# Second routing: the dense expert 0 becomes a routed expert, and 32 products of constants stand in the return's wait

## The reference

```python
logits = xf @ w_g                                   # 2048 x 8
topv, topi = jax.lax.top_k(logits, 2)
probs = softmax over the two chosen
capacity = int(2 * 1.25 * 2048 / 8)                 # 640
rank = cumsum over the first choices, then the second ones
mask = mask * (rank < capacity)
exp_batches = ... tokens of each expert, 8 x 640 x 128
h = gelu(exp_batches @ c_fc[e])                     # 128 -> 512
exp_out = h @ c_proj[e]                             # 512 -> 128
out = sum over the two experts, probability times exp_out
```

## Time and profile before

| what | value |
|---|---|
| median of 3 runs | 583.71 us (583.6 to 588.45) |
| span of the profiled execution, first to last instruction | 595.4 us |
| mean granted clock of TensorE over the span | 0.891 |
| PE busy | 505.9 us |
| DVE, ACT, POOL busy | 324.2, 239.9, 242.2 us |
| bytes moved, mean rate | 47.52 MB, 80 GB/s |

### The profile page before, as it was taken

One profiled execution on the slowest core, in us unless ns is written; L12 is line 12 of the kernel. 1 busy time (PEld: TensorE's weight loads), 2 busy tenths in 40 slices (PEclk: granted clock), 3 DMA queues, 4 the chain that ended last, 5 costly groups with the idle time before them and its releaser, 6 DMA issues.

```text
span 595.4 us, 9229 instructions
## 1 busy us (share of the span) xinstructions
PE 505.9 (85%) x3310; PEld 408.7 (69%) x3310; DVE 324.2 (54%) x1125; ACT 239.9 (40%) x477; POOL 242.2 (41%) x354
## 2 busy tenths in 40 slices
PE   3698993889769978978836799989899999999997
PEld 2557492778556626776725689988653779799997
DVE  4867338743896724598520246532774964433334
ACT  3643833233245541345520153322246187334430
POOL 5772957264334013475767306555390250000000
PEclk9799996569768998985668889999999799999999
DMA  9999801110850067400111122110800000000002
GB/s 285 334 176 196 260 34 35 37 39 28 294 153 1 1 185 219 128 1 2 44 46 48 44 68 65 55 35 24 274 2 0 2 1 2 0 1 1 1 2 70
DMA packets 55822, 47.52 MB, mean 80 GB/s; under 512 B 6059, under 2 KB 46201, under 8 KB 55649
## 3 DMA queue, kind: packets, MB, share of 16 engines
q1 hardware_dynamic: 52688, 41.54, 25.6%
q0 software_dynamic: 2656, 4.88, 2.6%
q10 hardware_dynamic: 432, 0.52, 0.3%
HBM read 34.69 MB, written 12.82 MB: 80 GB/s over the span
## 4 chain that ended last, share of the span: by engine, by line
PE 63%; DVE 20%; issue 4%; DMA 4%; POOL 3%; ACT 3%; another core or an unknown queue 3%; ACTq 0%; DVEq 0%; SPq 0%; POOLq 0%
PE ps L1244 10%; PE ps L1180 6%; PE ps L1063 4%; PE ps L1064 4%; PE ps L1065 4%; DVE st L1622 4%; PE ps L703 3%; PE ps L816 3%; PE ps L1091 2%; PE ps L756 2%; PE ps L746 2%; PE ps L839 2%; PE ps L819 2%; PE ps L1161 2%
## 5 line engine op out<-in xcount | busy, mean ns | idle before, releaser
L2047 DVE SCALAR_TENSOR_TENSOR x<-ps,gate,x 128x128 f32<-128x128 f32 x128 | 36.0, 345 | 54.8 <-PE ps L1244 54.8
L1244 PEld LDWEIGHTS ps<-moe_w,big 128*128 128x128 f32 x512 | 61.1, 192 | 3.9 <-issue 1.7
L2389 POOL DMA_INDIRECT res<-qT,dest x43 | 42.4, 986 | 49.0 <-DVE qT L2022 40.7
L1244 PE MATMUL ps<-moe_w,big 128*128 128x128 f32 x512 | 61.4, 275 | 0.9 <-DVE x L2036 0.9
L1509 ACT ACTIVATE big<-ps,col 128x512 f32<-128x512 f32 x64 | 42.3, 689 | 48.2 <-PE ps L1065 48.1
L703 PE MATMUL ps<-con,xn 128*128 128x128 f32 x148 | 28.6, 326 | 28.1 <-ACT xn L1447 15.7
L703 PEld LDWEIGHTS ps<-con,xn 128*128 128x128 f32 x148 | 20.4, 169 | 37.6 <-DVE xn L1640 34.8
L1180 PE MATMUL ps<-moe_w,big 128*128 128x128 f32 x344 | 42.8, 280 | 2.6 <-DVE qT L2022 2.0
L1359 ACT ACTIVATE xT<-ps 128x512 f32<-128x512 f32 x41 | 24.1, 590 | 49.9 <-PE ps L703 48.5
L1180 PEld LDWEIGHTS ps<-moe_w,big 128*128 128x128 f32 x344 | 40.9, 195 | 3.6 <-issue 2.2
L1501 ACT ACTIVATE big<-ps 128x320 f32<-128x320 f32 x56 | 23.5, 439 | 48.8 <-PE ps L1065 37.3
(11 more groups left out here) (346 smaller groups left out, 1215.8 us busy)
## 6 DMA issues: line engine op xcount, KB each, us to landing
ring<-in_ew SPq DMA_DIRECT2D x20, 256.0 KB, 5.0
moe_w<-in_m0w SPq DMA_DIRECT2D x16, 256.0 KB, 6.3
moe_w<-in_m2w SPq DMA_DIRECT2D x16, 256.0 KB, 5.4
tok<-zero SPq DMA_DIRECT2D x1, 2580.0 KB, 28.6
big<-tok SPq DMA_DIRECT2D x7, 322.5 KB, 3.1
res<-zero SPq DMA_DIRECT2D x1, 2048.0 KB, 29.4
moe_w<-in_ew SPq DMA_DIRECT2D x8, 256.0 KB, 5.5
big<-res SPq DMA_DIRECT2D x4, 512.0 KB, 6.5
```

Source lines behind the costliest of these rows:

```text
L1244: last = mm(ps[7 - i % 2 if i >= B else 6 + i % 2][:, cols(c)], big[:, FC * (e % 2) + f, i % B, cols(c)], w[:, e, F + P * f:F + P * f + P] ...
L2047: last = v.scalar_tensor_tensor(out=x[:, C * t + c, :], in0=bank[:, cols(c)], scalar=gate[:, C * t + c, e:e + 1], in1=x[:, C * t + c, :], ...
L2389: g_.indirect_dma_start(out=res_d[name], out_offset=bass.IndirectOffsetOnAxis(ap=dest[:, at:at + 1], axis=0), in_=ysb[:, i % 2, cols(b)], ...
```

## The change

Expert 0 is routed like the others. `whole_expert`, `whole_low_of`, `whole_out`, `have` and the stage `turn xs` go, on every engine; `placed` runs for eight experts instead of seven. Where tile 3 of expert 0 stood, PE now waits until the stores of the odd experts (the last of them is the last expert) have landed, and then runs 32 products of constants instead of 8. SP's wait ahead of the last layer's weight loads is for the last routed result. The lines cut here are declarations and the same change of index (`i + a["whole"]` to `i`).

```diff
@@ SEQ2
-        ("stats", "out2", "x", "also"), ("turn", "x", D, None, None), ("router", "wr2"), ("count", "m2"), ("place", "m2"), ("turn", "xs", D, None, None)]
+        ("stats", "out2", "x", "also"), ("turn", "x", D, None, None), ("router", "wr2"), ("count", "m2"), ("place", "m2")]
...
-BUSY_RETURN = 8
+BUSY_RETURN = 32
...
-        units0 = {"m0": 0, "whole": 4 * E, "m2": 4 * E + C * (B - 1)}
-        done0 = {"m0": 0, "whole": E, "m2": E + B - 1}
+        units0 = {"m0": 0, "m2": 4 * E}
+        done0 = {"m0": 0, "m2": E}
...
-        PLACED = {"m0": dict(cap=CAP0, eg=2, ranks=1, whole=0), "m2": dict(cap=CAP2, eg=1, ranks=2, whole=1)}
+        PLACED = {"m0": dict(cap=CAP0, eg=2, ranks=1), "m2": dict(cap=CAP2, eg=1, ranks=2)}
...
-            a["n"] = E - a["whole"]
+            a["n"] = E
@@ sync
-            sp.wait_ge(gy_mm, done0["last"] + 1)
+            sp.wait_ge(gy_mm, done0["last"])
             moe_load(sp, "m3", w3, 256, ld_m3)
@@ tensor, placed
                 if name == "m2":
                     pe.wait_ge(idx_ready, 2 * B)
-                    pe.wait_ge(x_high, 1)
                     count_second()
...
                 if name == "m2":
-                    whole_expert(loaded)
                     pe.wait_ge(idx_ready, 2 * B + 1)
                 for att in prepares:
                     prepare(att, keys_in)
@@ tensor, the engine's program
             placed("m2", 1, ld_m2, None, ["L3"])
-            whole_expert(ld_m2, True)
+            pe.wait_ge(gy_st[1], stores("m2", PLACED["m2"]["n"] // 2))
             keep_busy(ps[2], BUSY_RETURN)
             wavefront(make, SEQ3)
@@ scalar
-                    elif src == "xs":
-                        A(xT[:, t, :], ps[2 * t + 1][:, :], ACT.Identity).then_inc(xT_ready, 1)
-                        A(qTR[:, t, :], ps[2 * t + 1][:, :], ACT.Identity).then_inc(x_high, 1)
...
             chances()
-            whole_expert(ACT.Gelu, range(B - 1))
             placed("m2", 1, ACT.Gelu, None)
-            whole_expert(ACT.Gelu, (B - 1,))
             wavefront(make, SEQ3)
@@ vector, evacuate
                     if name == "m2":
-                        for c in range((nb - C) * i_ // a["n"], (nb - C) * (i_ + 1) // a["n"]):
-                            i = v.scalar_tensor_tensor(out=x[:, c, :], in0=whole_y[:, c, :], scalar=have[:, c:c + 1], in1=x[:, c, :],
-                                                       op0=ALU.mult, op1=ALU.add)
                         for j in range(2 * nb * i_ // a["n"], 2 * nb * (i_ + 1) // a["n"]):
@@ vector, the engine's program
-            whole_low_of(0)
-            whole_low_of(1)
             dve.wait_ge(gate_ep, 1)
             dve.wait_ge(cum_mm, 2 * B + 1)
...
-            link(v.tensor_tensor(have[:, 0:nb], gb[:, 0:nb, 0], gb[:, nb:2 * nb, 0], ALU.add))
-            whole_low_of(2)
-            whole_out(0)
-            whole_low_of(3)
-            for t in range(1, B - 1):
-                whole_out(t)
             prepared("L3")
             evacuate("m2", 1)
-            whole_out(B - 1)
-            dve.wait_ge(gy_sb, done0["last"] + 1)
-            for c in range(nb - C, nb):
-                i = v.scalar_tensor_tensor(out=x[:, c, :], in0=whole_y[:, c, :], scalar=have[:, c:c + 1], in1=x[:, c, :],
-                                           op0=ALU.mult, op1=ALU.add)
-            link(i)
             v.tensor_tensor(b2_blocks, bc(b2m3[:, :], [P, C, D], [1]), bc(K("chunk"), [P, C, D], [2]), ALU.mult)
```

More of the change, by code:

```diff
@@ L134, in told @@
 def told(k):
-    return sum(q not in ("x", "xs") for q in ALL_TURNS[:k])
+    return sum(q != "x" for q in ALL_TURNS[:k])
 def turns(k, t):
@@ L377, in build @@
         slot = sb("slot", [P, 2 * B * C])
-        have = sb("have", [P, 2 * B * C])
         wgt = sb("wgt", [P, 2 * B * C])
@@ L627, in placed_traffic @@
                         sp.wait_ge(gT_s, g0 + g - 1)
-                    rows = slice((a["whole"] + g) * a["gb"] * P, (a["whole"] + g + 1) * a["gb"] * P)
+                    rows = slice(g * a["gb"] * P, (g + 1) * a["gb"] * P)
                     sp.dma_start(xg[:, g % 2, 0:a["gb"] * (D + 1)].rearrange("p (b d) -> p b d", d=D + 1),
@@ L690, in stage @@
                         pe.wait_ge(sum_ready, 4 * raw_k + t - 3)
-                    elif src != "xs":
+                    else:
                         pe.wait_ge(tok_ready, 4 * tok + t + 1)
@@ L702, in stage @@
                         from_ = big[:, 0, t, cols(c)] if src == "soft" else source["xn" if mixes else src][:, C * t + c, 0:width]
-                        last = nc.tensor.transpose(ps[2 * t + (src == "xs")][:, cols(c)], from_, ident)
+                        last = nc.tensor.transpose(ps[2 * t][:, cols(c)], from_, ident)
                     last.then_inc(turned, 1)
@@ L1065, in product @@
                 mm(o, low, x_high_, start=False, stop=True).then_inc(h_mm, 1)
[L1067 to L1102, removed]
             def placed(name, k, loaded, bias, prepares):
@@ L1141, in hidden @@
                 def hidden(i, between=None):
-                    g, e = i // eg, i + a["whole"]
+                    g, e = i // eg, i
                     pe.wait_ge(gT_s, g0 + g + 1)
@@ L1170, in results @@
                 def results(i, units, blocks=range(nb)):
-                    e = i + a["whole"]
+                    e = i
                     pe.wait_ge(h_act, units)
@@ L1476, in chances @@
                 n["moe"] += 1
[L1478 to L1487, removed]
             def placed(name, k, fn, bias):
@@ L1960, in second_largest @@
                     link(i)
-            def whole_low_of(t):
-                dve.wait_ge(x_high, t + 1)
-                if t >= 2:
-                    dve.wait_ge(h_mm, units0["whole"] + C * (t - 1))
-                v.tensor_tensor(whole_low[:, t % 2, :], xT[:, t, :], qTR[:, t, :].bitcast(F32), ALU.subtract).then_inc(low_ready, 1)
-            def whole_out(t):
-                dve.wait_ge(gy_mm, done0["last"] + 1 if t == B - 1 else done0["whole"] + t + 1)
-                v.tensor_copy(whole_y[:, chunks(t), :], ps[6 + t % 2][:, :].rearrange("p (c d) -> p c d", c=C)).then_inc(gy_sb, 1)
             def evacuate(name, k):
@@ L1993, in group @@
                         number = xg[:, g % 2, 0:gb_ * (D + 1)].rearrange("p (b d) -> p b d", d=D + 1)[:, :, D]
-                        at = 40 + (a["whole"] + g) * gb_
-                        link(v.tensor_scalar(dest_f[:, g % 2, :], K("pos"), first_n[:, g + 1:g + 2], float(C), ALU.is_ge, ALU.mult))
+                        at = 40 + g * gb_
+                        link(v.tensor_scalar(dest_f[:, g % 2, :], K("pos"), first_n[:, g:g + 1], float(C), ALU.is_ge, ALU.mult))
                         i = v.tensor_tensor(dest[:, at:at + gb_], dest_f[:, g % 2, :], number, ALU.add)
@@ L2387, in deliver @@
                         pool.wait_ge(gy_sb, done0[name] + i * a["nb"] + b + 1)
-                        at = (40 if seen else 0) + (i + a["whole"]) * a["nb"] + b
+                        at = (40 if seen else 0) + i * a["nb"] + b
                         g_.indirect_dma_start(out=res_d[name], out_offset=bass.IndirectOffsetOnAxis(ap=dest[:, at:at + 1], axis=0),
```

8 lines of the change are left out of this document (3 added, 5 removed).

## The result

The changed kernel takes 597.97 us (median of 4 runs, 595.79 to 599.25), the kernel before beside it 583.71 us (583.6 to 588.45): 1.0232 times as long, with a 95% interval of 1.0195 to 1.0269. On another chip it took 596.68 against 585.31 us, 1.0208 [1.0184, 1.0232]. The forecast was 596.2 us, slower.

What follows compares the result with a forecast made beforehand. PE was taken to bound the kernel wherever it has work; dense tiles 0, one more expert 8.6 and the return 3.9 sum to 12.5 us, added to 583.7 for 596.2 us, 2.1% slower; range 588 to 600.

Steps and rivals of the forecast that it cites:

- The stalls belong to the recorded execution: Send's wait and 396.95: PE, DVE and ACT stalls taken as that recording's only; 13.5 us left out of the base.
- Dense tiles at 0: Send's wait: removing expert 0's dense tiles 0 to 2 saves 0, being beside POOL's sends; bounds 0 and -7.7 us.
- `turn xs` at 0: Send's wait: removing this stage's 16 transposes and 8 copies saves 0, since POOL's trains begin on their own order.
- One more expert at 8.64: Routed experts: an eighth one lengthens PE's steady state by 8.64 us; bounds 8.5 to 8.9.
- The return at +3.9: Last result to sums: 4.9 us idle, then 32 products in 8.7 us; net +3.9, bounds +2.1 and +4.8.
- the 8 to 9.5 us that the prediction named as its sign: Return, profile after: 32 products should take this long, with a granted clock of 0.50 at first.
- The 0.8 us that a wait in the sums was to give back: Sums: loads land before the later first sum, so PE's 0.80 us wait at 421.86 goes.
- ACT's table load: Ahead of the first gelu: stays in the send's wait at 0, or +1.3 us if it came after it.
- The profiled span of about 600: Whole recording after: span grows by about 4.8 us, to 600, since a send's-wait stall no longer holds PE up.
- The upper end of the terms: Whole kernel: the terms' ends give 594.3 to 598.7 us, to 600 with the table load.
- Case C: Return: all 32 products stay at half clock, 14.0 us instead of 8.7, total 601.5 us; chance 0.09.
- Case B: Send's wait and routed experts: the dense expert causes stalls in every run; removing it gives 580.9 us, faster; chance 0.05.

Runs made afterwards that it cites:

- the kernel before again: The kernel before, unchanged, timed and recorded a second time: 586.23 us, ratio 1.0021 to the kernel before timed beside it.

## Why the prediction was right

Compared inside like recordings, the kernel before again and after:

| stretch | before again | after | difference | predicted |
|---|---|---|---|---|
| first send to first hidden product | 51.4 | 51.0 | -0.4 | 0 |
| first hidden product to last result | 63.1 | 71.5 | +8.4 | +8.6 |
| last result to first sum | 10.4 | 14.6 | +4.2 | +4.7 |
| first sum to end | 175.0 | 175.8 | +0.8 | -0.8 |

The rows add up to +13.0 us, predicted +12.5. The timed difference was 14.3 us on the first chip and 11.4 on the second; these lie further apart than any error of a term, so the account of the terms rests on the recordings.

*The stalls belong to the recorded execution:* shown, and with it the main choice of the prediction, its base. Neither the kernel before again nor any of the other recordings has them, the transposes stand where the schedule without stalls put them, and taking the dense tiles away changed nothing. The 11.7 us between profile and median was the evidence that counted. What brings such stalls on stays open; no run had them again. So nothing was learned about the Trainium skill's rule on the ports ("SBUF — State Buffer", ports) beyond what the prediction says: in the kernel before again, DVE's longest waits beside POOL's sends are of 4.40, 5.06 and 2.88 us, and all three are ended by PE's results.

*Dense tiles at 0:* right, by the experiment that removes them. PE loses 19.3 us of busy time, and the path none. *`turn xs` at 0:* right as far as the recordings show, since the distance from the first send to the first hidden product stays within 0.4 us; the stage wasn't tried by itself.

*One more expert at 8.64:* right. In the chain of the kernel after, sets of results begin 8.57 us apart:

```profile
344.80 4.47 PE ps L1137 x40
...
353.37 4.47 PE ps L1137 x40
```

The next ones begin at 361.94, 370.50 and 379.07. Leaving an expert out takes 8.6 us out of the stretch.

*The return at +3.9:* the steps were right and the size was too small; that the table has +4.2 beside +4.7 is luck, two errors against each other. The steps: 4.93 us of idle time for 4.9 predicted, half clock at the start of the products, no wait for a load. But the products took 9.80 us, not 8.7, and so lie outside the 8 to 9.5 us that the prediction named as its sign. At full clock they take 7.07, so 2.7 us are the clock's price, 5.5 us or so of half clock where I had assumed 3.5; the lower figure was a choice between 0 and the 5.3 us of the earlier trace rows, and the row was the better guide. With that the first sum comes 14.57 us after the last result, 5.7 later than the 8.9 of the earlier trace rows, where 4.7 was predicted. And the 8.9 isn't what the kernel before always has: in its other recording it is 10.40, since the last store lands 1.7 us later behind an instruction fetch, and with this base the difference is only 4.2. The 0.8 us that a wait in the sums was to give back are there in part against the first recording (176.3 us from the first sum to the end, 175.8 after), and not against the other, which has no such wait (175.0). The return with what follows costs 5.0 us against the one and 5.2 against the other, for 3.9 predicted. The recording that the prediction read has the fetch too, 1.9 us after the last store's issue, but all of the store's packets are ahead of it (the DMA view of that recording, 414.3 to 415.2 us):

```profile
DMA packets 33, 0.04 MB, mean 47 GB/s; under 512 B 24, under 2 KB 24, under 8 KB 32
...
q0 software_dynamic: 32, 0.03, 10.4%
q8 instruction: 1, 0.02, 7.0%
```

So the base of 8.9 was one that the kernel before has only when the store just comes first. How often the timed runs have the one or the other isn't known.

*ACT's table load:* it moved, into the first hidden product of the first expert (the timeline of ACT after):

```profile
334.63 1.28 ACT L1444 ACT_TABLE_LOAD   x1 [40.87 <-PE ps L1061]
335.93 1.50 ACT L1444 ACTIVATE big<-ps 128x320 f32<-128x320 f32 x4
```

It was loaded by the dense expert's first gelu in the wait for the sends, and that is gone. I had it at 0 there or at +1.3. It did come late, but PE had four blocks of passes at half clock ahead of it and never waited for the gelu: 0 for another reason.

*The profiled span of about 600:* wrong, 595.2. I let the stall at 396.95 and the gap in POOL's train stand in the recording after, though I held them to be that one execution's. Consistently, it was 581.9 + 12.5 = 594.4.

*The upper end of the terms:* added up wrongly. The upper bounds give 583.7 + 8.9 + 4.8 = 597.4 us; 598.7 has the 1.3 us of the table load in it already, and 600 has it twice. The median of 597.97 us lies just above the 597.4.

*Case C* (all products at half clock) is out: the clock returns some 5.5 us after the products start. *Case B* is out with the stalls.

A version faster than both came out of the study: the kernel before with 54 + 10 products of constants, 580.66 us against 584.93, 0.9927 [0.9902, 0.9953]. Its recording, beside that of the kernel before again, puts 0.4 us of that ahead of the first hidden product, 1.5 in the first expert and 1.5 in the return; the last is an accident of where an instruction fetch falls.

## What to carry to other kernels

Work in a wait is free only until the wait is over: three dense tiles beside the sends cost nothing, and the same expert, routed after them, costs 8.6 us, though PE has less to do in all. Products of constants are free while they end before the wait does: 32 beside the stores, or 8 behind them that were done before the load landed, cost nothing, and 32 behind the stores outlasted the load and cost 5 to 6.5 us. Before terms are read from one recording, hold its span against the median of the timed runs; where they part by 11.7 us, look for the stretch that makes the difference and take it out of the base.

## What the runs showed of the hardware that I had not expected

- A wait of PE of only 2.37 us, after 13.76 us of unbroken products at full clock and the transposes, is followed by some 3.4 us at 0.50 in the first expert (passes of 0.27 us instead of 0.15); filling it with 10 products takes 1.5 us off the path. After 4.93 us of idle time the half clock lasted some 5.5 us into the products.
- A packet of 16 KB of an instruction queue that comes ahead of a store's last two small packets goes with a landing after 3.7 to 3.8 us instead of 2.1. With 24 products more in PE's program it came elsewhere. So an edit far from the return can change the return by 1.6 us. The Trainium skill, "Runtime: NRT & Kernel Launch", in its section on instruction fetch, says that instructions come in blocks of 16 KiB (256 of them) over a DMA queue and that the cost of a block is mostly hidden. The size agrees with the packet (0.02 MB on its own queue). That the cost is hidden may hold for PE, for which no wait shown here is put down to it; it doesn't hold for the store beside it.
- One execution of the kernel before had PE, DVE and ACT standing still beside POOL's trains and 4.0 us in the routed experts, and was some 12 us longer. That is open.
